# A decoder layer on one core: queries and keys in two float32r parts instead of three bf16 parts, with the scores paired on the array's halves

## The reference

```python
q = (x @ Wq + bq).reshape(B, S, N_HEADS, D_K).transpose(0, 2, 1, 3)
k = (x @ Wk + bk).reshape(B, S, N_HEADS, D_K).transpose(0, 2, 1, 3)
v = (x @ Wv + bv).reshape(B, S, N_HEADS, D_K).transpose(0, 2, 1, 3)
scores = jnp.einsum('bhsd,bhtd->bhst', q, k) * scale
attn = jax.nn.softmax(scores, axis=-1)
ctx = jnp.einsum('bhst,bhtd->bhsd', attn, v)
...
x = x + 0.5 * _L0_ffn_ref(_layernorm(x, axis=-1), ...)
x = x + _L0_attn_ref(_layernorm(x, axis=-1), ...)
x = x + 0.5 * _L0_ffn_ref(_layernorm(x, axis=-1), ...)
```

## Time and profile before

| | us |
|---|---|
| median of 3 runs | 1001.35 (998.92 to 1003.1) |
| the profiled execution's own span | 996.9 |
| PE busy | 907.5 |
| DVE busy | 832.2 |
| ACT busy | 750.2 |
| POOL busy | 219.1 |

### The profile page before, as it was taken

The page is one execution under the profiler, slowest core; times in us unless marked ns, Lnnn a source line. Parts: engine busy times, 40 slices in busy tenths (PEclk is TensorE's granted clock), DMA queues, the critical chain, the costliest instruction groups (busy, mean ns, idle before and its releaser), DMA issues. The chain is left out here.

```text
span 996.9 us, 18005 instructions
## 1 busy us (share of the span) xinstructions
PE 907.5 (91%) x5949; PEld 385.6 (39%) x6023; DVE 832.2 (83%) x1404; ACT 750.2 (75%) x1507; POOL 219.1 (22%) x317
## 2 busy tenths in 40 slices
PE   5799927899999999999999999999999999965996
PEld 4699923322222222222222222222222222434996
DVE  6776628989999999999999999999999998768664
ACT  4367706978888888888888888888888888754774
POOL 3168841831000000000000100000100000024775
PEclk9989957999999999999999999999999999996998
DMA  7632135752220213202022120220202000051311
GB/s 262 194 96 73 41 116 190 238 192 63 58 61 16 62 34 81 62 17 62 15 73 74 31 62 15 73 54 28 75 30 64 29 23 17 2 169 48 105 63 44
DMA packets 65443, 75.14 MB, mean 75 GB/s; under 512 B 12896, under 2 KB 43784, under 8 KB 65352
## 3 DMA queue, kind: packets, MB, share of 16 engines
q1 hardware_dynamic: 58776, 60.98, 20.6%
q0 software_dynamic: 5120, 12.59, 4.1%
q10 hardware_dynamic: 1456, 0.41, 0.2%
HBM read 40.47 MB, written 33.49 MB: 74 GB/s over the span
## 5 line engine op out<-in xcount | busy, mean ns | idle before, releaser
L1574 DVE TENSOR_REDUCE maxima<-ps_m 128x2 f32<-128x1024 f32 x512 | 602.8, 1221 | 53.8 <-PE ps_m L1335 52.8
L1544 ACT ACTIVATE probs<-ps_s 128x512 f32<-128x512 f32 x1024 | 555.9, 600 | 109.5 <-PE ps_s L1381 77.7
L1381 PE MATMUL ps_s<-q,k 74*128 74x512 bf16 (+1 forms) x950 | 294.5, 385 | 3.0 <-ACT probs L1544 0.9
L1392 PE MATMUL ps_o<-probs,vs 128*32 128x512 f32 x2048 | 272.7, 605 | 0.7 <-ACT probs L1544 0.7
L1381 PEld LDWEIGHTS ps_s<-q,k 74*128 74x128 bf16 (+1 forms) x1024 | 79.5, 97 | 303.4 <-ACT probs L1544 217.1
L1335 PE MATMUL ps_m<-k,q 64*128 64x512 bf16 x1024 | 159.9, 385 | 13.8 <-ACT probs L1544 7.9
L1265 POOL TENSOR_SCALAR split<-top 128x16 bf16<-128x16 f32 x32 | 8.1, 253 | 445.8 <-DVE top L1590 428.7
L1335 PEld LDWEIGHTS ps_m<-k,q 64*128 64x128 bf16 x1024 | 49.1, 93 | 102.7 <-issue 58.1
L693 PE MATMUL ps_y<-W,hT 128*128 x624 | 83.8, 278 | 0.0
L1392 PEld LDWEIGHTS ps_o<-probs,vs 128*32 128x32 f32 x2048 | 40.3, 108 | 109.3 <-issue 95.1
L693 PEld LDWEIGHTS ps_y<-W,hT 128*128 128x128 f32 x624 | 77.0, 194 | 0.6 <-issue 0.4
(11 more groups left out here) (215 smaller groups left out, 586.3 us busy)
## 6 DMA issues: line engine op xcount, KB each, us to landing
k_rows<-parts SPq DMA_DIRECT2D x24, 384.0 KB, 4.5
sums<-oT SPq DMA_DIRECT2D x30, 256.0 KB, 3.6
q<-q_parts SPq DMA_DIRECT2D x75, 96.0 KB
k<-k_rows SPq DMA_DIRECT2D x15, 288.0 KB
token_rows<-x SPq DMA_DIRECT2D x16, 256.0 KB, 4.1
token_rows<-v_and_ctx SPq DMA_DIRECT2D x16, 256.0 KB, 3.6
k<-k_rows SPq DMA_DIRECT2D x15, 256.0 KB
q_parts<-parts SPq DMA_DIRECT2D x8, 384.0 KB, 3.4
```

The costliest lines, as they stand in the source:

```text
L1381: nc.tensor.matmul(ps_s[n % 3][:, :], k2[buffer(g)][0:contracted, j, kt * P:(kt + 1) * P], q2[buffer(g)][0:contracted, j, u * HALF:(u + 1) ...
L1392: last = nc.tensor.matmul(ps_o[32 * j:32 * (j + 1), :], vs[buffer(g)][:, kt, j, :], probs[:, s % 2, j, :], start=(kt == 0), stop=(kt == KT ...
L1544: nc.scalar.activation(probs[:, s % 2, j, :], ps_s[n % 3][:, :], ACT.Exp, scale=SCALE).then_inc(exped, 1)
L1574: nc.vector.tensor_reduce(maxima[:, :, pr, qt, kh], ps_m[slot][:, :, :], AX.X, ALU.max).then_inc(unit_free[slot], 1)
```

## The change

Queries and keys are split into two float32r parts (float32r is a float32 that TensorE reads at reduced precision), with four products of 8 rows, so 32 rows for a head. With one row of constants and two guards that makes 35 rows, and two heads fit above each other: the even head at row 0, the odd one at row 64 (`ODD`). A score contracts 35 rows in one half of the array, a unit 33 rows in each half. The second part is now one instruction on DVE for every quad, straight from the bank; ACT's `exact` and second parts and all subtractions of POOL are gone. The fills become five for a buffer, of which four are 2048 columns wide. The key parts are stored once, and a group is loaded with 4 and 8 DMAs (before: 7 and 3).

```diff
-PARTS = 3
+PARTS = 2
 ROWS = PARTS * PARTS * DK
-MAX_ROWS = ROWS - DK
+ODD = P // 2
 GUARDS = 2
-SCORED = ROWS + GUARDS
+GUARD = ROWS + 1
+SCORED = GUARD + GUARDS
...
+    PIECES = 5
+    FILLED = PIECES * BUFS
 
     def gpsimd_fill(self, pool, n):
...
-        p, piece = n // 4, n % 4
+        p, piece = n // self.PIECES, n % self.PIECES
         if n:
             pool.wait_ge(self.filled, n)
-        if piece == 0:
-            self.nc.gpsimd.memset(self.k2[p][64:96, 0::2, :].bitcast(F32), self.PAIR).then_inc(self.filled, 1)
-        if piece == 1:
-            self.nc.gpsimd.memset(self.k2[p][0:64, 1::2, :].bitcast(F32), self.PAIR).then_inc(self.filled, 1)
-        if piece == 2:
-            self.nc.gpsimd.memset(self.q2[p][0:64, 1::2, :].bitcast(F32), 0.0).then_inc(self.filled, 1)
-        if piece == 3:
+        if piece < 2:
+            self.nc.gpsimd.memset(self.k2[p][piece * ODD + ROWS:piece * ODD + SCORED, :, :].bitcast(F32), 1.0).then_inc(self.filled, 1)
+        elif piece < 4:
+            start = (piece - 2) * ODD + ROWS
+            self.nc.gpsimd.memset(self.q2[p][start:start + 1, :, :].bitcast(F32), 0.0).then_inc(self.filled, 1)
+        else:
             self.nc.gpsimd.memset(self.vs[p][:, :, :, :], 1.0).then_inc(self.filled, 1)
 
     def tensor_biases(self, pe):
@@ -885,7 +886,7 @@
...
-        LOADS, STORES = 2 * PARTS + 1 + 3, 1 + PARTS
+        LOADS, STORES = 2 * PARTS + 2 * PARTS * PARTS, 2
...
-                    for j in (2 * pr, 2 * pr + 1):
-                        rows = slice(j % 2 * MAX_ROWS, (j % 2 + 1) * MAX_ROWS)
-                        last = nc.tensor.matmul(ps_m[slot][:, j % 2, :], q2[buffer(g)][rows, j, qt * P:(qt + 1) * P],
-                                                k2[buffer(g)][rows, j, kh * HALF:(kh + 1) * HALF], start=True, stop=True)
+                    for j in range(2):
+                        rows = slice(j * ODD, j * ODD + GUARD)
+                        last = nc.tensor.matmul(ps_m[slot][:, j, :], q2[buffer(g)][rows, pr, qt * P:(qt + 1) * P],
+                                                k2[buffer(g)][rows, pr, kh * HALF:(kh + 1) * HALF], start=True, stop=True)
...
-                    for unit in units:
+                    for unit in units[:1]:
                         do_unit(*unit)
-                    for j in range(GH - 1):
+                    for j in range(2):
                         score(g, k, j)
+                    for unit in units[1:]:
+                        do_unit(*unit)
+                    score(g, k, 2)
                     if s:
                         values(s - 1)
                     score(g, k, GH - 1)
...
-                    if FIRST <= q < LAST:
-                        nc.scalar.activation(exact[:, q % 2, j, :], bank[:, :], ACT.Identity, bias=bias[:, 0:1]).then_inc(high, 1)
-                    nc.scalar.activation(parts[:, q % SPLITS, j, 0, :], bank[:, :], ACT.Identity, bias=bias[:, 0:1]).then_inc(high, 1)
+                    nc.scalar.activation(parts[:, q % SPLITS, j, 0, :].bitcast(F32R), bank[:, :], ACT.Identity, bias=bias[:, 0:1]).then_inc(high, 1)
...
-                    dve.wait_ge(high, high_parts(q) + j + 1)
-                    nc.vector.scalar_tensor_tensor(out=rem[:, q % 2, j, :], in0=bank[:, :], scalar=bias[:, 0:1], in1=parts[:, q % SPLITS, j, 0, :],
-                                                   op0=ALU.add, op1=ALU.subtract).then_inc(left[q % LAST], 1)
+                    dve.wait_ge(high, 2 * q + j + 1)
+                    nc.vector.scalar_tensor_tensor(out=parts[:, q % SPLITS, j, 1, :].bitcast(F32R), in0=bank[:, :], scalar=bias[:, 0:1],
+                                                   in1=parts[:, q % SPLITS, j, 0, :], op0=ALU.add, op1=ALU.subtract).then_inc(left, 1)
...
+                held, late, units = [], [], 0
+
+                def behind(items):
+
+                    for kind, n in items:
+                        if kind == "value":
+                            values(n)
+                        else:
+                            remainder(n, int(kind == "key"))
...
+                    if kind in ("query", "key", "value") and n >= FIRST:
+                        late.append((kind, n))
...
+                        behind(held)
+                        held, late = late, []
+                behind(held + late)
```

More of the change, by code:

```diff
@@ L6 @@
 BF16 = mybir.dt.bfloat16
+F32R = mybir.dt.float32r
 I32 = mybir.dt.int32
@@ L887 @@
 FIRST = 2
-SPLITS = 3
+SPLITS = 2
 SOFT = STEPS * GROUPS
@@ L982, in attention @@
         top, negated = (sb(name, [P, 2, GH // 2 * QUAD], F32) for name in ("top", "negated"))
-        split = sb("split", [P, 2, GUARDS, GH // 2 * QUAD], BF16)
-        blocks = [sb(f"blocks{p}", [P, 4 * KT], BF16) for p in range(2)]
+        split = sb("split", [P, 2, GUARDS, GH // 2 * QUAD], F32)
+        blocks = [sb(f"blocks{p}", [P, 4 * KT], F32) for p in range(2)]
         ps_m = [ctx.enter_context(nc.psum_tensor(f"ps_m{p}", [P, 2, HALF], F32)) for p in range(2)]
@@ L1012, in use, with product @@
             return g // BUFS
[L1014 to L1020, removed]
+        def product(j, n):
+            return j % 2 * ODD + n * PARTS * DK
         def load_queries(engine, g, landed, tokens=slice(0, SEQ)):
@@ L1036, in load_keys @@
             for j in range(2):
[L1037 to L1046, removed]
+                k_rows = dram["k_parts"][b, :, :, slice(first + j, first + GH, 2), tokens]
+                for n in range(PARTS):
+                    for m in range(PARTS):
+                        row = product(j, n) + m * DK
+                        engine.dma_start(k[row:row + DK, :, tokens].bitcast(F32), k_rows[n, :, :, :]).then_inc(landed, 16)
         def where(q):
@@ L1074, in stores_landed, with parts_done @@
                 engine.wait_ge(query_stored, 16 * (q + 1))
[L1076 to L1081, removed]
+        def parts_done(engine, q, count):
+            engine.wait_ge(left, 2 * q + count)
         def landed_results(q):
@@ L1088, in landed_results @@
             return 16 * (GROUPS - 1 + GPB - 1)
[L1090 to L1099, removed]
-            p = q % 2
-            engine.wait_ge(middle, 2 * q + j + 1)
-            nc_engine.tensor_tensor(parts[:, q % SPLITS, j, 2, :], rem[:, p, j, :], parts[:, q % SPLITS, j, 1, :], ALU.subtract).then_inc(low[0 if q == LAST else min(q, FIRST)], 1)
         norm = Norm(nc, w["x"], xn_sb, stats, mv, rt, vstep, astep, normed)
@@ L1500, in high_both @@
                         high_part(q, j)
-                def second_part(q, j):
-                    parts_done(act, left, q, j + 1)
-                    nc.scalar.activation(parts[:, q % SPLITS, j, 1, :], rem[:, q % 2, j, :], ACT.Copy).then_inc(middle, 1)
                 front.scalar(act)
@@ L1716, in _ @@
                             finish_scales(3)
-                        while late:
-                            values(late.pop(0))
-                parts_done(dve, low, LAST - 2, 2)
-                for j in range(2):
-                    remainder(LAST, j)
-                while late:
-                    values(late.pop(0))
-                for j in range(2):
-                    third_part(dve, nc.vector, LAST, j)
+                        behind(held)
+                        held, late = late, []
+                behind(held + late)
                 for s, units in enumerate(SCHEDULE):
```

97 lines of the change are left out of this document (28 added, 69 removed).

## The result

The changed kernel takes **1401.01 us** (median of 4 runs, 1399.15 to 1406.69), against 1000.3 us (998.92 to 1003.1, 4 runs) for the kernel before: a ratio of 1.400, 95% interval 1.397 to 1.404. Forecast were 960 us and, at most, 1080.

The account below looks back on a forecast made before the run. PE was taken as the bound, DVE next. Loop -60, fills +13 and projections +5 gave -42 us, so 1001.35 us would become 959, stated as 960; the range was 941 to 1080.

Parts of the forecast that it names:

- the bf16 pace, 0.22: Loop, PE: a float32r matmul of 512 columns was taken to cost 0.22 us, like bf16.
- PE's sum of 2.20 us: Loop: units, scores and values of one step need 2.20 us on PE, 0.42 less than before.
- The last eleven steps: Loop's end, 844 to 878 us: a full-array matmul replaces the units; no gain or loss counted.
- float32r's pace: Loop's units and scores: float32r makes one pass, with one record for a matmul and 0.22 us between single ones.
- The second rival: Loop: float32r costs fp32's 0.45 a pass, pairs still at once; 1087 to 1197 us in all; chance 0.10.
- The first rival: Loop: the array's halves don't run at once with float32r; step 2.86, 1077 us in all; chance 0.12.
- the third rival: Loop: weight loads no longer hide; step 2.53 to 2.86, 995 to 1077 us in all; chance 0.08.
- the break-even of 2.55: Loop: the step in us below which the change wins, with 18 us to be paid back.
- DVE's floor and the gap: Loop: DVE becomes the bound at 2.30 a step, with some gap left 2.38; gain 60 us, from 40 to 75.
- Fills: POOL's queue ahead of attention: wider and additional fills delay the load of x, +13 us, from +9 to +14.
- The fourth rival: Fills: the loop is faster but 2048 columns cost no more than 1024; 950 us, inside the forecast's 0.66.
- Projections: Projections ahead of the loop: DVE gains second parts; +5 us, from +2 to +9.

Follow-up runs that it names:

- run 2: Changed kernel, float32r kept, with scores and units widened to 64 rows a half by ones against zeros: 1021.61 us.
- kernel 10: The kernel of run 2 with 13 of its 15 fills moved into POOL's idle time ahead of the gathers: 1004.49 us.
- run 6: Changed kernel in float32r with only the scores widened to 64 rows a half, units still at 33: 1023.94 us.
- run 7: Changed kernel in float32r with scores and units widened to 48 rows a half: 1030.56 us.
- run 3: Changed kernel with the old order: two units together, three scores, the values, the last score: 1392.61 us.
- kernel 12: The kernel of run 5 with 13 of its 15 fills moved into POOL's idle time: 1020.05 us, ratio 0.968 to the kernel before.
- run 11: As kernel 10, with the fourth score right behind the third, ahead of the values: 1078.46 us.
- run 5: Changed kernel with bf16 in place of float32r and 64 rows a half: 972.99 us, ratio 0.972 to the kernel before.
- run 4: Kernel before with only its fills changed, to five a buffer, four of them 2048 columns wide: 1012.65 us.

## Why the prediction was wrong

**The step that failed** is the one that every term of the loop was built on and that the prediction never weighed: the slots were priced at "the bf16 pace, 0.22", which is the pace at a granted clock of 1.00, read from rows in which a matmul contracts 64 to 128 rows. The change cuts that to 33 and 35 a half. PE's sum of 2.20 us then holds only at the high level; the loop ran at 0.50, with a step of 4.07. What the runs showed in its place: the level is low at the loop's beginning in every kernel of the new layout, after PE's idle gaps, and the rows decide whether it comes back. In float32r it is back after 7 us with 64 rows (runs 2, 10), after 14 with the scores alone at 64 (run 6), after 17 with 48 (run 7), and with 35 not within the loop's 1022 us, in either order (the changed kernel, run 3). That the level depends on the rows in use is shown. That the operand type matters too is shown as well: at 35 rows bf16 got the level back after some 190 us in both traces, and the mean clocks of its five runs (0.815 to 0.915) lie far above those of float32r's five (0.582 to 0.595). Why rows and type have this effect is open. The products of the added rows are all zero, so it isn't the sums that count; more than this no run says. No rival had the clock in it, so the range didn't either.

**Of the 380 us in the loop** between the first and the last values, the steps give (4.07 - 2.624) x 243 = 351. The last eleven steps, counted at nothing, give 29 at the low level (5.74 instead of 2.86 for most). At 1.00 they give 2.5 (kernel 10) and 0 (kernel 12): the zero was right for its clock.

**float32r's pace.** Right: one pass, one record, one column a cycle. The second rival falls: slots are 0.43 us at 1.2 GHz, and at 1.00 they are 0.24 apart, where bf16 has the forecast 0.22 (run 11: scores at 500.86, the next unit at 501.10). With it falls, as a limit of bytes, the 614 GB/s of the Trainium skill, SBUF — State Buffer ("A bandwidth-pool intuition that's wrong"). With what the Trainium skill says under FP8 and Floating Point Precision, TensorE Precision Notes, that reduced precision reads four bytes and truncates, where true fp32 takes four passes, the trace agrees: one record and 0.24 us for a matmul of 512 columns.

**Pairs** start at once. The first rival falls.

**Weights that no longer hide:** the third rival was partly right, and this is the second error. In run 2 a float32r load of 128 columns takes 185 ns, in run 5 a bf16 load 94:

```profile
L1333 PEld LDWEIGHTS ps_s<-q,k 64*128 64x128 f32 x459 | 75.9, 185 | 147.9 <-ACT probs L1481 144.1
```

About 0.1 of it stands open at the third score and at the fourth. Both lie on the ring that sets the step: fourth score, its exponential, the third score that waits for the bank, the values, the fourth score again. Once around it in run 2:

```profile
502.78 0.50 PE L1333 MATMUL ps_s<-q,k 64*128 64x512 f32 x1
503.31 2.06 ACT L1481 ACTIVATE probs<-ps_s 128x512 f32<-128x512 f32 x4 [0.54 <-PE ps_s L1333]
503.96 0.49 PE L1333 MATMUL ps_s<-q,k 64*128 64x512 f32 x1
504.38 1.07 PE L1344 MATMUL ps_o<-probs,vs 128*32 128x512 f32 x8
505.38 0.50 PE L1333 MATMUL ps_s<-q,k 64*128 64x512 f32 x1
```

That is 0.53 + 0.65 + 0.42 + 1.00 = 2.60; in run 5 the same four terms are 0.42 + 0.65 + 0.32 + 1.00 = 2.39. In float32r DVE's 2.36 are no longer the bound, and the common step of 2.61 is above the break-even of 2.55. So the change in float32r would have been slower even at the full clock: run 2, its counterpart at 1.00, takes 1022 us in its one execution. This is inside the range, but on the wrong side.

**DVE's floor and the gap:** 2.38 was forecast as the mean step, and the mean in runs 5 and 12 is 2.44 (2.39 in six steps of eight), so the loop gives 44 us and not 60, inside the forecast 40 to 75. Two things were missing. The ring of 2.39, as long as DVE's two reductions with their small gap, wasn't seen: that the common step lies so near to 2.38 is luck. And two waits of every eight steps, for the guards and for `oT`, which the longer step of before had nearly hidden (its mean is 2.625 at a common step of 2.62), were counted at nothing.

**Fills:** +13 forecast; the load of x is 13.3 later, and run 4 gives 12.8 by the time of the whole kernel. The fourth rival falls. **Projections:** +5 forecast; 18.2 - 13.3 = 4.9.

## What to carry to other kernels

A change that makes matmuls use fewer rows can take away the clock at which they were priced: before summing PE's instructions, ask what the array does less of, and put the loop at half clock among the rivals, with its price. Ask two things of a low level: what PE did before it fell, and why it doesn't rise. If it stays low in a busy loop, rows of zeros are the cheapest test and may be the cure. And where an instruction waits on one of several banks, follow every bank's ring; the one that has slack may owe it to work that happens to stand in front.

## What the hardware showed that I had not expected

- The granted clock stayed at 0.50 for the whole loop, with PE busy for 1022.58 of 1022.60 us. The Trainium skill (TensorE: Matmul & The Clock Gate, Part 1: The HAM clock gate) has the clock set by how busy PE has been, with the low level for an idle engine. The fall agrees with it, behind idle gaps of 1.80 and 0.83 us; that the level never rose does not, if busy is read as the busy time of the profile.
- Adding rows of zeros made the kernel 379 us faster. With bf16 at 35 rows the level rises in the middle of a uniform loop, at a moment that differs from run to run, and the same kernel takes from 1000.68 to 1078.66 us.
- GpSimd's fills hold up some DVE operations: 32 bf16 `TENSOR_SCALAR` of 128 columns took 9.89 us under fills and 5.29 without, an int32 cast 1.80 instead of 0.18, ending with the fill. DVE's float32 operations beside fills kept their length (`upto`, L404: 0.69 in runs 2 and 10). The Trainium skill (SBUF — State Buffer, SBUF: two separate sides) calls the ports that the two engines share an exclusive lock, held for a whole instruction, for those DVE operations that use two ports. The trace agrees: three `TENSOR_SCALAR` start during a fill and all end just behind it. Which operations use two ports is in no view here.
- A fill costs by its columns and not by its partitions: 2048 columns take 1.80 us on 3 partitions and on 32, 1024 columns 0.95 on 32 or on 128.
